# VectorE takes three of seven chunks of logits out of the accumulators in the first step of a two-step graph layer

## The reference

```python
def _adj_from_feats(Xa, W1, W2, W3):
    Q = Xa @ W1
    K = Xa @ W3
    logits = Q @ W2 @ K.T / TAU
    idx = jnp.argsort(-logits, axis=1)
    vals = jnp.take_along_axis(logits, idx, axis=1)
    csum = jnp.cumsum(jax.nn.softmax(vals, axis=1), axis=1)
    k_i = jnp.sum(csum < P_NUC, axis=1) + 1
    ...
    masked = jnp.where(keep, logits, -jnp.inf)
    return jax.nn.softmax(masked, axis=1)
...
for s in range(STEPS):
    A = _adj_from_feats(Xa, W1, W2, W3)
    Xf = Rf @ Xf
    Xb = Rb @ Xb
    Xa = A @ Xa
    Z = Z + (Xf @ U1[s] + Xb @ U2[s] + Xa @ U3[s])
```

## Time and profile before

| | us |
|---|---|
| median of 3 runs | 2548.35 (2547.64 to 2549.64) |
| the profiled execution, its own time | 2547.09 |
| its span, first to last instruction | 2545.3 |
| TensorE busy | 2224.6 |
| VectorE busy | 2076.8 |
| ScalarE busy | 2000.3 |
| mean granted TensorE clock, as a share of full speed | 0.94 |

### The profile page before, as it was taken

How to read it: one execution, slowest core, us unless ns; L and a number is a source line. 1 busy time by engine, 2 the same in 40 slices (tenths; PEclk the granted TensorE clock), 3 DMA queues, 4 the chain that set the end, 5 groups by cost and what they waited for, 6 DMA issues and landing times. The chain is left out here.

```text
span 2545.3 us, 25834 instructions
## 1 busy us (share of the span) xinstructions
PE 2224.6 (87%) x8302; PEld 1423.5 (56%) x8302; DVE 2076.8 (82%) x3829; ACT 2000.3 (79%) x3021; POOL 377.1 (15%) x661
## 2 busy tenths in 40 slices
PE   7588888888888887899759999999999999999846
PEld 4366666666666666444325555555555555555535
DVE  4689888988888888244499999999999999999733
ACT  5799999999999985233688898989898898989413
POOL 2121222112221221000011111111111111111100
PEclk9699999999999998899769999999999999999968
DMA  5234443444434431321102211121222112122141
GB/s 202 59 80 113 116 100 87 106 114 102 96 94 114 113 90 36 99 63 42 56 18 49 51 48 38 49 51 47 49 51 49 40 54 44 47 49 51 22 133 54
DMA packets 77980, 183.18 MB, mean 72 GB/s; under 512 B 11665, under 2 KB 57872, under 8 KB 77840
## 3 DMA queue, kind: packets, MB, share of 16 engines
q1 hardware_dynamic: 56800, 125.48, 15.5%
q0 software_dynamic: 18720, 54.53, 12.6%
q10 hardware_dynamic: 2320, 1.48, 0.2%
HBM read 154.19 MB, written 27.28 MB: 71 GB/s over the span
## 5 line engine op out<-in xcount | busy, mean ns | idle before, releaser
L1392 DVE SCALAR_TENSOR_TENSOR s_junk<-s_logits,s_small,s_expd 128x3327 uint8<-128x3327 f32 x208 | 766.3, 3684 | 4.6
L935 PE MATMUL bank<-h_aug,s_attT 128*128 128x256 f32 x2704 | 625.8, 380 | 28.8 <-ACT s_attT L1161 28.8
L911 PE MATMUL bank<-both,s_adj 128*128 128x512 f32 x1352 | 619.3, 607 | 0.0
L935 PEld LDWEIGHTS bank<-h_aug,s_attT 128*128 128x128 f32 x2704 | 500.9, 190 | 134.8 <-ACT s_attT L1161 41.6
L911 PEld LDWEIGHTS bank<-both,s_adj 128*128 128x128 f32 x1352 | 259.0, 196 | 277.8 <-issue 275.0
L899 PE MATMUL bank<-KTr,QT 64*128 64x512 f32 (+1 forms) x728 | 293.5, 686 | 137.2 <-ACT s_logits L1030 136.3
L911 PE MATMUL bank<-h_aug,s_adj 128*128 128x257 f32 x1352 | 324.1, 391 | 9.4 <-ACT s_spread_out L1168 9.4
L1094 ACT ACTIVATE s_junk<-s_expd,s_small 128x3327 int8<-128x3327 f32 x104 | 319.2, 3069 | 1.8
L1098 ACT ACTIVATE s_junk<-s_expd,s_small 128x3327 int8<-128x3327 f32 x104 | 319.8, 3075 | 1.0
L911 PEld LDWEIGHTS bank<-h_aug,s_adj 128*128 128x128 f32 x1352 | 252.5, 193 | 89.9 <-issue 45.0
L1030 ACT ACTIVATE s_logits<-bank 128x512 f32<-128x512 f32 (+1 forms) x364 | 190.1, 565 | 115.9 <-PE bank L899 115.8
(11 more groups left out here) (215 smaller groups left out, 2250.4 us busy)
## 6 DMA issues: line engine op xcount, KB each, us to landing
s_adj<-adj_turned SPq DMA_DIRECT2D x104, 832.0 KB, 5.3
s_adj_total<-adj_turned POOLq DMA_DIRECT2D x52, 832.0 KB, 10.0
z<-s_sides_out POOLq DMA_DIRECT2D x52, 128.0 KB, 3.3
spread<-s_spread_out SPq DMA_DIRECT2D x26, 128.5 KB, 2.9
m_spread_in<-spread SPq DMA_DIRECT2D x26, 128.5 KB, 2.2
attended<-s_att_out SPq DMA_DIRECT2D x26, 128.0 KB, 1.7
m_att_in<-attended SPq DMA_DIRECT2D x26, 128.0 KB, 2.2
z<-m_z_out SPq DMA_DIRECT2D x26, 128.0 KB, 1.7
```

The lines of the kernel that those rows point to most:

```text
L911: done = pe.matmul(SX[:, 0:width], half(t, h)[:, bass.ts(jj, P)], rows_of(j), start=(j == 0), stop=(j == T - 1))
L935: last = pe.matmul(AB[:, 0:D], attT[i % 4][:, b, :], h_aug[:, g + b, 0:D], start=(g + b == 0), stop=(g + b == T - 1))
L1392: chain.did(dve.scalar_tensor_tensor(junk[:, 0:N], logits[t % 3][:, 0:N], col(t, "cand"), expd[t % NE][:, 0:N], ALU.is_gt, ALU.mult, accum ...
```

## The change

In step one, `copied` is 4: ScalarE copies chunks 0 to 3 and VectorE takes chunks 4 to 6. VectorE's row maximum has three parts: a reduction of the 2048 copied columns, then for each of the three chunks a `tensor_scalar` that reads the accumulator, writes the logits to SBUF and leaves the largest value of the chunk, then a reduction over the four values. A new semaphore, `logits_taken`, tells TensorE that these accumulators are free. Three memsets set the padding column.

The order of the other engines in step one changes as well. TensorE transposes four groups before its spread group 5, and places the products and the spread group 6 anew among the rest. ScalarE takes the transposed groups 0 to 3 between the two passes of the first probe, 4 and 5 behind it, 6 in the second probe, and reads the spread accumulator after the probes. In step two nothing changes.

```diff
--- before.py
+++ after.py
@@ -765,6 +765,7 @@
         def step(number, both):
             first_step = number == 0
             early, late = EARLY[number], LATE[number]
+            copied = 4 if first_step else NC
             tag = f"s{number}_"
             with ExitStack() as c:
                 def sbt(name, shape, dt=F32):
@@ -812,6 +813,9 @@
                     n = 48 + 2 * PAIRS.index("point0")
                     return small[t % 3][:, n + 1:n + 4:2]
 
+                def highest(t, n=None):
+                    return small[t % 3][:, 84:88] if n is None else small[t % 3][:, 84 + n:85 + n]
+
                 def mask(t):
                     return masks[t % 3][:, :]
 
@@ -829,7 +833,7 @@
                          "turned_stored", "attended_groups", "spread_read", "att_read", "setup", "constants_set", "dve",
                          "act", "low_ready", "pool", "settled", "larger_summed"]
                 if first_step:
-                    names += ["adj2_loaded", "adj3_loaded", "adj_added", "spread_stored0", "spread_stored1",
+                    names += ["adj2_loaded", "adj3_loaded", "adj_added", "logits_taken", "spread_stored0", "spread_stored1",
                               "att_stored0", "att_stored1"]
                 else:
                     names += ["adj_checked", "keys_summed", "keys_folded", "keys_ready", "rows_added0", "rows_added1",
@@ -892,7 +896,11 @@
                             at, w = s.CHUNKS[n]
                             i = t * NC + n
                             if i >= 2:
-                                pe.wait_ge(sem["logits_stored"], i - 1)
+                                earlier, chunk = divmod(i - 2, NC)
+                                if chunk < copied:
+                                    pe.wait_ge(sem["logits_stored"], earlier * copied + chunk + 1)
+                                else:
+                                    pe.wait_ge(sem["logits_taken"], earlier * (NC - copied) + chunk - copied + 1)
                             if i == NC - 1 and not first_step:
                                 pe.wait_ge(sem["keys_ready"], 1)
                             r = (n % 2) * DA
@@ -959,23 +967,24 @@
                             if following:
                                 make_logits(t + 1, range(4, NC))
                             if present:
-                                for n in range(2, 6):
+                                for n in (2, 3, 4):
                                     spread(t, n)
                             if previous:
-                                for n in range(3):
+                                for n in range(4):
                                     turn(t - 1, n)
+                            if present:
+                                spread(t, 5)
+                            if previous:
+                                turn(t - 1, 4)
+                                turn(t - 1, 5)
+                                multiply(t - 1, 0)
+                                turn(t - 1, 6)
+                                multiply(t - 1, 1)
+                                multiply(t - 1, 2)
                             if present:
                                 spread(t, 6)
                             if previous:
-                                turn(t - 1, 3)
-                                turn(t - 1, 4)
-                                multiply(t - 1, 0)
-                                multiply(t - 1, 1)
-                                turn(t - 1, 5)
-                                multiply(t - 1, 2)
-                                multiply(t - 1, 3)
-                                turn(t - 1, 6)
-                                for n in range(4, NG):
+                                for n in range(3, NG):
                                     multiply(t - 1, n)
                         else:
                             if following:
@@ -1193,7 +1202,7 @@
                         pass
 
                     act.wait_ge(sem["constants_set"], 5)
-                    store_logits(0, range(NC))
+                    store_logits(0, range(copied))
                     exponentials(0)
                     guess(0)
                     for k in range(early):
@@ -1211,25 +1220,18 @@
                             if previous:
                                 count_ties(t - 1)
                             if following:
-                                store_logits(t + 1, range(2, NC))
+                                store_logits(t + 1, range(2, copied))
                             if previous:
                                 lift(t - 1)
                             if following:
                                 exponentials(t + 1)
                                 guess(t + 1)
-                            turned(0, 1)
-
-                            def amid_first():
-                                turned(2)
-                                if present:
-                                    read_spread(t)
-                                turned(3, 4)
-                            if following:
-                                probe(t + 1, 0, amid_first, lambda: turned(5))
+                                probe(t + 1, 0, lambda: turned(0, 1, 2, 3), lambda: turned(4, 5))
                                 probe(t + 1, 1, lambda: turned(6), nothing)
                             else:
-                                amid_first()
-                                turned(5, 6)
+                                turned(0, 1, 2, 3, 4, 5, 6)
+                            if present:
+                                read_spread(t)
                             if previous:
                                 read_attended(t - 1)
                         else:
@@ -1335,9 +1337,25 @@
                     chain = Steps(dve, sem["dve"])
 
                     def row_max(t):
-                        dve.wait_ge(sem["logits_stored"], (t + 1) * NC)
-                        chain.did(dve.tensor_reduce(col(t, "max"), logits[t % 3][:, 0:N], AX.X, ALU.max))
-                        chain.wait()
+                        dve.wait_ge(sem["logits_stored"], (t + 1) * copied)
+                        if first_step:
+                            chain.did(dve.tensor_reduce(highest(t, 0), logits[t % 3][:, 0:s.CHUNKS[copied][0]],
+                                                        AX.X, ALU.max))
+                            for n in range(copied, NC):
+                                at, w = s.CHUNKS[n]
+                                w = min(w, N - at)
+                                i = t * NC + n
+                                dve.wait_ge(sem["logits_done"], i + 1)
+                                dve.tensor_scalar(logits[t % 3][:, at:at + w], LB[i % 2][:, 0:w], 1.0, None,
+                                                  ALU.mult, ALU.max, accum_out=highest(t, n - copied + 1)
+                                                  ).then_inc(sem["logits_taken"], 1)
+                            dve.wait_ge(sem["logits_taken"], (t + 1) * (NC - copied))
+                            chain.wait()
+                            chain.did(dve.tensor_reduce(col(t, "max"), highest(t), AX.X, ALU.max))
+                            chain.wait()
+                        else:
+                            chain.did(dve.tensor_reduce(col(t, "max"), logits[t % 3][:, 0:N], AX.X, ALU.max))
+                            chain.wait()
                         if not first_step:
                             chain.did(dve.tensor_scalar(col(t, "over_mean"), col(t, "max"), logits[t % 3][:, N:NP],
                                                         -math.log(1 - P_NUCLEUS), ALU.subtract, ALU.add))
@@ -1492,7 +1510,9 @@
                         dve.memset(expd[i][:, N:NP], -1.0).then_inc(sem["setup"], 1)
                     for i in range(3):
                         dve.memset(best(i, 3)[:, 0:1], 0.0).then_inc(sem["setup"], 1)
-                    dve.wait_ge(sem["setup"], 2 * late + 4 + NE)
+                        if first_step:
+                            dve.memset(logits[i][:, N:NP], 0.0).then_inc(sem["setup"], 1)
+                    dve.wait_ge(sem["setup"], 2 * late + 4 + NE + (3 if first_step else 0))
                     if not first_step:
                         pad = keys_of(NG - 1, NP - (NG - 1) * 512)[:, N - NP:]
                         chain.did(dve.tensor_tensor(fold[:, :], ident[:, 0:DA], ident[:, DA:P], ALU.add))
```

## The result

The changed kernel takes 2491.49 us (median of 4 runs, 2489.55 to 2493.39) against 2547.99 for the kernel before beside it; the ratio is 0.9779, 95% interval 0.9763 to 0.9794. It was forecast faster, at 2482 with a range of 2469 to 2506. The direction and the range held; the gain is 56 us where 66 were forecast. The profiled execution has a span of 2488.9, against 2545.3.

A forecast was written before the change was run, and what follows sets the result against it. No single bound before; after the change VectorE sets step one's tile. 23 tiles at 2.58 us less (59.3), plus 1.9, 2.2, 2.0 and 1.0 at the ends, give 66.4 off 2548.35: 2482, range 2469 to 2506.

The forecast's parts named there:

- The sum of a tile: Step one: VectorE's work and waits in one tile add to 33.33 us against 35.91, 2.58 less.
- M: The moment in each tile when VectorE's row maximum is done and the largest value is ready; repeated every 35.91 us.
- it is the bound: Step one's tile: VectorE has almost no idle time left after the change and sets the tile at 33.33 us.
- the tie of chunk 3: Before the reduction: ScalarE's copy of chunk 3 (about M+28.6) and VectorE's first weighing (M+28.54) end together.
- The takes of 512 columns: VectorE's row maximum: each read of a 512-column chunk from an accumulator costs 0.70 us, from copies of 687 ns.
- so nothing is late: TensorE after chunk 6: three spread groups end at new M+4.4, the kept row comes at M+4.3, so no delay.
- 1.9 to spare: End of TensorE's tile: multiplies done at M+21.3, attended rows wanted at M+23.2, slack 1.9 us.
- the rival of late ties: ScalarE or TensorE comes late to a tie; 0.5 us per tile gives 2494, 1.0 gives 2507; chance 0.13.
- another rival: TensorE's clock falls in its new waits; decides above 6 us of slowed work per tile, about 2600 with 10; chance 0.05.
- the rival that the reduction isn't brought forward: Spread group 0 behind ScalarE's reading makes chunks 2 and 3 late; tile stays 35.9, time 2540 to 2550; chance 0.04.
- The ends: Outside the 23 middle tiles: gains of 1.9, 2.2 and 2.0 us before tile 2, 1.0 after the last search.
- The note on the accumulators: VectorE pays 120 fixed cycles from an accumulator, 58 from SBUF; three takes would be 1.71 us, the whole 2479.

The follow-up runs named there:

- e9: e1 with row-maximum reduction split in two, spread accumulator read in second probe, only three of spread group 2's four matmuls before chunk 6: 2471.42 us.
- e1: The changed kernel, but TensorE does spread group 2 between chunks 5 and 6 of the logits: 2480.31 us.
- e6: e1, with ScalarE also reading the spread accumulator in the second probe, ahead of transposed group 6: 2478.9 us.
- e8: e1, but ScalarE copies five chunks and VectorE takes two: 2510.46 us.
- e2: The changed kernel with TensorE's and ScalarE's orders put back to those of the kernel before; VectorE still takes chunks 4 to 6: 2580.82 us.
- e5: e2, but TensorE does spread group 2 between chunks 5 and 6: 2502.26 us.
- e3: The changed kernel's orders of TensorE and ScalarE only; ScalarE copies all seven chunks and VectorE reduces 3327 columns: 2539.13 us.

## Why the prediction was right, and where it was off

**The sum of a tile held, the bound only nearly.** Wherever the clock stays up the tile is 33.24, against 33.33 forecast. Its terms: from M to the next search 23.65 (23.79 forecast), from there to the reduction 5.10 (4.87), the row maximum 4.49 (4.67). Chunk 3, which the walk tied with the weighing, lands where it was put: the reduction starts 28.75 after M, 28.66 forecast. But VectorE is ready at 28.36, not at 28.54, and the 0.39 between makes ScalarE's chain the one that sets this tile, together with the row maximum; "it is the bound" holds for VectorE only once its waits are cut to 0.18 (e9). e1 and e6 show the tile of 33.24 almost without exception, and e8 shows that the tie of chunk 3 is a real one.

**The takes of 512 columns were priced 0.10 too high each.** They follow on each other by 0.60, where 0.70 was taken from copies of 687 ns. The single row is 0.68 to 0.69, close to those copies, but the next take begins before its end, and the accumulator read of 0.08 lies within that.

**The term that failed is TensorE's.** The prediction saw the 1.7 us in front of chunk 6 (1.87 measured) and costed it at nothing, with "so nothing is late" and 1.9 to spare at the end. At the full clock its walk was right to 0.1: the three groups end at M+4.4 and the products at M+21.4 (21.3 forecast). But the 1.9 was reckoned to the attended rows. The next tile's first chunk stands behind them on TensorE, and there the rows leave only about 1.0: chunk 0 reaches ScalarE 1.22 after its start in the slow tile (542.99 to 544.21), so after a start at 406.55 it would be there at 407.77, and ScalarE took it at 408.81. The prediction held that a fall of the clock decides only at over 6 us of work at the lower level, and gave it 0.05. A fall far short of that already has a price: about 1.6 us of delay uses up the slack, and what is left reaches ScalarE as 0.45 and VectorE as 0.96 instead of 0.39. Over 23 tiles it is 23 x (33.69 - 33.24) = 10.4 us. The span missed by 10.0 (2488.9, where 2545.3 - 66.4 = 2478.9 was forecast), but that the two agree is in part luck: the fast tile was 2.1 cheaper over 23 tiles and the start 0.2, the end was 1.9 dearer, and these nearly cancel. In size the lateness is what the rival of late ties had for 0.5 per tile (2494), and the range, drawn wide enough for that rival, covered it. The mechanism was under another rival, and the two were one: a clock that falls for a few microseconds makes TensorE late to a tie. The 23 tiles of the changed kernel show it, fall by fall, and e1 shows that filling the gap takes the whole of it away. The rule of the Trainium skill's page "TensorE: Matmul & The Clock Gate" (its section on a second failure mode), that short idle times between groups of matmuls can make the clock swing, was dismissed because no tile of the kernel before showed it. The rows after bear it out for this kernel, in 17 tiles of 23 (0.95 over one tile, 1.00 over another with the same gap).

**The change does two things that need each other as long as the gap is open.** Of the rival that the reduction isn't brought forward, e2 shows the form that was not seen: the takes with the old orders bring it forward and lose more at the transposes. The orders alone give 8 us, the takes alone lose 33, both give 56. With the gap filled the takes alone give 45 (e5), and the orders 22 on top.

**The ends.** The 6.1 up to tile 2 came as 6.31. Behind the last search a gain of 1.0 was forecast and 0.9 was lost, 0.34 of it up to the sums of the columns; the rest lies behind them and is not traced here. The prediction let ScalarE's earlier start bring `keep` forward. It is GpSimd that ends last there. In the last tile of the kernel after its rows are:

```profile
915.94 3.45 POOL L1271 TENSOR_TENSOR s_small<-s_small 128x1 f32<-128x1 f32 x1
...
921.53 0.34 POOL L1291 TENSOR_SCALAR s_small<-s_small 128x1 f32<-128x1 f32 x1
```

VectorE's weighing starts sooner after the end of its previous tile, and in the rows it is GpSimd's third operation that is as long as the weighing, where it was the fourth before, so one more operation stands behind it. The result is ready 6.66 after the start of the search instead of 6.30, and `keep` starts 7.40 after it instead of 7.04. In the middle tiles this is hidden, as forecast. The GpSimd operations beside the reduction took 0.21 to 0.34, so it doesn't hold them.

**The note on the accumulators.** By the Trainium skill's page "VectorE: DVE Perf Modes" (the section on the TRN2 errata) a take of 512 columns would be 658 ns, an estimate worked out from its figures. The rows say 0.68 to 0.69, and 0.60 from start to start. Its point that the work moves to the engine that reads accumulators at the worse price is true here (0.60 against ScalarE's 0.54, from start to start) and did not matter, since ScalarE's copies stood on the path and VectorE's waiting time paid for the takes.

What stays open is why the same gap of 1.87 is followed by a fall in 17 tiles and by none in six; no run here varied its length alone.

## What to carry to other kernels

When a change makes TensorE wait for one more engine, put work that is ready into the new gap, and price a fall of its clock even where the gap itself has slack: the gap was 1.87 us, and a fall behind it mostly cost 1.7 more. Reckon the slack to the next thing that anyone waits for, here the next tile's first chunk and not only the result. When two engines meet at a tie, moving one of them gains nothing until the work around the tie is cut to fit, here one matmul. And moving work between engines and reordering them may be worth little or less than nothing one by one, so each part should be walked with the other undone.

## What the runs showed of the hardware

The granted clock fell behind idle stretches of 1.87 us in 17 of the 23 tiles, to 0.66 as a mean of the stretch from 518.57 to 522.00, and stayed at 1.00 in six tiles with the same stretch. In e3, 3.20 of idle time was followed by 16 transposes in 3.54 or in 1.97, and in e8 2.55 by 3.62 or 1.97. The kernel before had 1.46 in front of its transposes in each tile and no fall. A `tensor_scalar` of VectorE that reads an accumulator, writes SBUF and keeps a maximum costs 0.60 us per 512 fp32 columns in a row of such takes, and 0.42 for 255 columns as a single row. A GpSimd operation that takes 0.19 us alone (946.43 in the kernel after) took 3.45 beside a VectorE instruction with two SBUF inputs.
